# Expert routing and row scatter moved into the first attention layer's pipeline, in batches of four tiles

## What is computed

```
def _L0_ffn_ref(x, W1, b1, W2, b2, Wr, br):
    ...
    logits = xf @ Wr + br
    gates = jax.nn.softmax(logits, axis=-1)
    top_g, top_i = jax.lax.top_k(gates, K)          # E = 8, K = 2
    for e in range(E):
        w_e = jnp.sum(top_g * (top_i == e), axis=-1)
        h = jax.nn.gelu(xf @ W1[e] + b1[e], approximate=False)   # D = 192, I = 768
        out = out + w_e[:, None] * (h @ W2[e] + b2[e])
```

## Time and profile before

| | |
|---|---|
| median of 3 runs | 2311.49 us (2299.59 to 2316.12) |
| the profiled execution | 2312.43 us, span 2310.7 us |
| PE busy | 1958.2 us (85%) |
| DVE busy | 1397.8 us (60%) |
| ACT busy | 1011.0 us (44%) |
| POOL busy | 578.5 us (25%) |
| granted TensorE clock, mean | 0.914 of 2.4 GHz |

### The profile page before, as it was taken

The page is one execution under the profiler, slowest core; times in us unless marked ns, Lnnn a source line. Parts: engine busy times, 40 slices in busy tenths (PEclk is TensorE's granted clock), DMA queues, the critical chain, the costliest instruction groups (busy, mean ns, idle before and its releaser), DMA issues. The chain is left out here.

```text
span 2310.7 us, 57088 instructions
## 1 busy us (share of the span) xinstructions
PE 1958.2 (85%) x18472; PEld 1776.6 (77%) x18472; DVE 1397.8 (60%) x3149; ACT 1011.0 (44%) x2767; POOL 578.5 (25%) x1167
## 2 busy tenths in 40 slices
PE   5999999999500058999999999699999999999985
PEld 4888888888400058999999999588888888888872
DVE  5777777776432224555555554477777777777735
ACT  2555555555200022333333333366666666666631
POOL 4343333432057700000000000433333333333100
PEclk8999999999655578999999999599999999999957
DMA  4122222221012279788888886465555555555513
GB/s 130 56 58 59 62 55 62 56 60 34 10 59 78 78 197 267 219 239 234 235 235 235 235 233 200 118 179 163 160 158 157 156 162 162 162 161 159 152 30 109
DMA packets 377119, 322.00 MB, mean 139 GB/s; under 512 B 55432, under 2 KB 337760, under 8 KB 377058
## 3 DMA queue, kind: packets, MB, share of 16 engines
q1 hardware_dynamic: 357592, 287.49, 43.8%
q0 software_dynamic: 15360, 31.48, 4.5%
q10 hardware_dynamic: 4106, 2.24, 0.4%
HBM read 209.51 MB, written 111.60 MB: 139 GB/s over the span
## 5 line engine op out<-in xcount | busy, mean ns | idle before, releaser
L1122 ACT ACTIVATE prob<-ps_s,b1s 128x256 f32<-128x256 f32 x432 | 181.3, 471 | 371.6 <-PE ps_s L1106 371.6
L1106 PE MATMUL ps_s<-xhi,w1hi_c 128*128 128x256 f32 x864 | 240.1, 296 | 2.6 <-DVE xhi L1144 2.6
L1106 PE MATMUL ps_s<-xhi,w1lo_c 128*128 128x256 f32 x864 | 230.3, 284 | 0.0
L1081 PE MATMUL ps_v<-probT,prob 128*128 128x192 f32 x864 | 214.8, 331 | 0.0
L1069 PE MATMUL ps_t<-ident,xs 128*128 128x128 f32 x144 | 38.8, 295 | 207.2 <-DMA score<-w1h 206.4
L1081 PE MATMUL ps_k<-probT,prob 128*128 128x192 f32 x864 | 214.0, 330 | 0.0
L1136 DVE CAST w1hi_c<-score 128x768 fp32r<-128x768 f32 x144 | 74.1, 557 | 225.3 <-DMA score<-w1h 225.3
L371 PE MATMUL ps_k<-xT,wqk_c 128*128 128x128 f32 (+1 forms) x1408 | 198.7, 291 | 0.6 <-ACT xT L606 0.6
L422 PEld LDWEIGHTS ps_v<-vv,probT 128*128 128x128 f32 x1536 | 189.1, 199 | 1.1 <-issue 1.0
L422 PE MATMUL ps_v<-vv,probT 128*128 128x17 f32 x1536 | 187.7, 262 | 0.5 <-DVE hres L674 0.5
L1069 PEld LDWEIGHTS ps_t<-ident,xs 128*128 128x128 f32 x144 | 20.7, 144 | 215.3 <-DMA score<-w1h 206.0
(11 more groups left out here) (207 smaller groups left out, 4757.2 us busy)
## 6 DMA issues: line engine op xcount, KB each, us to landing
rel_d<-rpad SPq DMA_DIRECT2D x64, 864.0 KB, 4.4
relb<-rel_d SPq DMA_DIRECT2D x64, 768.0 KB, 5.1
probT<-w2h SPq DMA_DIRECT2D x72, 576.0 KB, 4.2
score<-w1h SPq DMA_DIRECT2D x72, 384.0 KB, 3.2
score<-w1h SPq DMA_DIRECT2D x144, 192.0 KB, 3.9
xs_d<-zrow SPq DMA_DIRECT2D x64, 216.0 KB
xs<-xs_d SPq DMA_DIRECT2D x72, 192.0 KB, 2.5
ys_d<-ys SPq DMA_DIRECT2D x72, 192.0 KB, 5.1
```

Of the source, the lines that this page charges most:

```text
L1081: last = pe.matmul(ps_y[s][:, 0:D], hT[b][:, c, s * 128:s * 128 + 128], w2[b][:, c, :], start=(c == 0), stop=(c == NI - 1))
L1106: last = pe.matmul(dst, w, x, start=(k == 0), stop=(k == len(terms) - 1))
L1122: last = act.activation(hT[b][:, c, :], ps_s[:, j, (c % 2) * BLK:(c % 2) * BLK + BLK], ACT.Gelu, bias=b1s[b][:, c:c + 1])
```

## The change

Blocks B and C are gone. Their work is done in block A for four tiles at a time:

- The ages grow to gate 11, pick 12, count 13, place 14, row 17, scatter 18; 20 steps are written out ahead of the loop instead of 12, and 18 behind it instead of 10. What is done for four tiles at once stands in every fourth step.
- DVE: `subtract_maximum` (2 instructions), `pick_experts` (15) and `place_rows` (9) stand at the end of a step's body, each once in four steps, on 128x32 or smaller operands. PE: `count_experts`, five matmuls behind the second half of the scores, which wait for `pick_experts`. ACT: an exponential of 128x32, a copy of the counts, and per tile the normalised row `srow` (before, DVE's work in block C). POOL: per tile two index copies and the two indirect stores, behind `rsz` and ahead of the next gather.
- Each expert has a fixed region of 8448 rows in `xs_d`, so that a row's place is known before all tokens are counted. The zeros written per tile are gone; four stores at the start zero 2048 spare rows, and eight at the start of block D zero the 256 rows behind each expert's last (`zero_tails`, on SP and ACT).
- Block D begins with a chain of DVE instructions for the tables `etabi` (expert) and `otabi` (first row of the block); SP now reads a second register per block, from `otabi`, behind the wait for the buffers. Packing the row numbers for the second layer and turning them is done in the first steps of block D.

```diff
+CAP = T * B + BLK
+ROWS = E * CAP + E * BLK
...
-AGES = [dict(gather=0, emb=1, ln=2, xn=3, qk=4, v=5, s=5, pt=6, o=7, y=8, z=9, lg=10),
+AGES = [dict(gather=0, emb=1, ln=2, xn=3, qk=4, v=5, s=5, pt=6, o=7, y=8, z=9, lg=10,
+             gate=11, pick=12, count=13, place=14, row=17, scatter=18),
...
+                if l == 0 and st.has("scatter"):
+                    t, j = st.tile("scatter"), st.four("scatter")
+                    after(pool, scat[j], 32 * st.quad("scatter"))
+                    pool.wait_ge(R_["placed"], st.quad("scatter") + 1)
+                    for k in range(TOPK):
+                        settle(pool, spare)
+                        pool.tensor_copy(sidx[j][k][:], posi[k][:, bass.ds(t, 1)]).then_inc(R_["idx"], 1)
+                    pool.wait_ge(R_["idx"], TOPK * upto(t))
+                    pool.wait_ge(R_["row"], upto(t))
...
+                        pool.indirect_dma_start(xs_d, bass.IndirectOffsetOnAxis(ap=sidx[j][k][:], axis=0),
+                                                srow[j][:], None).then_inc(scat[j], 16)
...
+                def count_experts():
+                    pe.wait_ge(R_["hots"], st.quad("count") + 1)
...
+                    pe.matmul(ps_t[:, 0:4 * E], tri_r[:], both_r[:], start=True, stop=False)
+                    for k in range(1, 4):
+                        pe.matmul(ps_t[:, k * E:4 * E], ones_r[:], both_r[:, 0:(4 - k) * E], start=False, stop=False)
+                    pe.matmul(ps_t[:, 4 * E:8 * E], ones_r[:], both_r[:], start=False, stop=True)\
...
+                if l == 0 and st.ends_quad("gate"):
+                    act.wait_ge(R_["less_max"], st.quad("gate") + 1)
+                    act.activation(gate4[:], gate4[:], ACT.Exp).then_inc(R_["gates"], 1)
+                if l == 0 and st.has("row"):
...
+                    act.activation(srow[j][:].rearrange("p (o d) -> p o d", o=1), hres[:, bass.ds(t, 1), :],
...
+                def pick_experts():
...
+                    rc.link(dve.tensor_reduce(gsum[:], gate4[:], AX.X, ALU.add))
+                    settle(dve, spare)
+                    rc.link(dve.reciprocal(gsum[:], gsum[:]))
+                    settle(dve, spare)
+                    rc.link(dve.tensor_tensor(gate4[:], gate4[:], wide(gsum[:]), ALU.mult))
+                    for k in range(TOPK):
+                        best, hot = quad_of("pick", wk[k]), one_hot[k]
+                        settle(dve, spare)
+                        rc.link(dve.tensor_reduce(best, gate4[:], AX.X, ALU.max))
+                        settle(dve, spare)
+                        rc.link(dve.tensor_tensor(hit[:], gate4[:], wide(best), ALU.is_equal))
+                        rc.link(dve.tensor_tensor(hit[:], hit[:], every(rev[:]), ALU.mult))
+                        settle(dve, spare)
+                        rc.link(dve.tensor_reduce(quad_of("pick", chosen[k]), hit[:], AX.X, ALU.max))
+                        settle(dve, spare)
+                        rc.link(dve.tensor_tensor(hot[:], hit[:], wide(quad_of("pick", chosen[k])), ALU.is_equal))
+                        if k == 0:
+                            rc.link(dve.scalar_tensor_tensor(gate4[:], hot[:], -2.0, gate4[:], ALU.mult, ALU.add))
+                    dve.tensor_tensor(both_r[:].rearrange("p (t e) -> p t e", e=E), one_hot[0][:], one_hot[1][:],
+                                      ALU.add).then_inc(R_["hots"], 1)
...
+                if l == 0 and st.ends_quad("gate"):
+                    subtract_maximum()
+                if l == 0 and st.ends_quad("pick"):
+                    pick_experts()
+                if l == 0 and st.ends_quad("place"):
+                    place_rows()
             pipeline(dve, ages, body, ch, 10 if l == 0 else 7)
...
+            for n in range(E * BLK // (128 * ZROWS)):
+                sp.dma_start(spare_rows[n], zrow[:, 0:ZROWS * D]).then_inc(xs_zero, 16)
...
-                    sp.dma_start(zr[bass.ds(t, 1)].rearrange("o p d -> (o p) d"), zrow[0:zr.shape[1], 0:ZROWS * D])\
-                        .then_inc(xs_zero, 16)
...
+                def block_row(t):
+                    return sp.value_load(otabi[0:1, bass.ds(t, 1)], min_val=0, max_val=ROWS - BLK)
...
                         after(sp, D_["h_sb"], NH * before2)
                         settle(sp, spare)
-                        rows_ = xs_d[bass.ds(t * BLK, BLK), :].rearrange("(s p) d -> p s d", s=2)
+                        rows_ = xs_d[bass.ds(block_row(t), BLK), :].rearrange("(s p) d -> p s d", s=2)
```

More of the change, by code:

```diff
@@ L237, in tower @@
         oT1 = two("oT1", [D1 + 1, 128])
-        srow = xn + zn
+        srow = four("srow", [128, D])
+        gate4 = sb("gate4", [128, 4, E])
+        gsum = sb("gsum", [128, 4])
+        hit = sb("hit", [128, 4, E])
+        one_hot = [sb(f"one_hot{k}", [128, 4, E]) for k in range(TOPK)]
+        both_r = sb("both_r", [128, 4 * E], F32R)
+        ranks = sb("ranks", [128, 8 * E])
+        place4 = sb("place4", [128, 4, E])
+        taken = sb("taken", [128, E])
+        filled = sb("filled", [128, E])
+        first_row = sb("first_row", [128, E])
+        rev = sb("rev", [128, E])
         w1 = [[score[p][:].rearrange("p g a k -> p (g a k)")[:, c * I:(c + 1) * I] for c in range(2)]
@@ L273, in tower @@
         xs_zero = sem("xs_zero")
+        scat = [sem(f"scat{p}") for p in range(SCAT)]
         rel_zero = sem("rel_zero")
@@ L278, in tower @@
                  "mvz_ok", "rsz_ok", "zn_ok", "zT_ps", "zT_sb", "lg_ps", "lg_sb")
+        R_ = {n: sem("R_" + n) for n in ("table", "dve", "less_max", "gates", "hots", "ranks_ps", "ranks_sb", "placed",
+                                         "row", "idx")}
         L = [{n: sem(f"L{l}_{n}") for n in NAMES} for l in range(2)]
@@ L571, in body @@
                                    ACT.Copy).then_inc(S["q_sb"], 1)
+                if l == 0 and st.ends_quad("count"):
+                    act.wait_ge(R_["ranks_ps"], st.quad("count") + 1)
+                    after(act, R_["placed"], st.quad("count"))
+                    act.activation(ranks[:], ps_t[:, 0:8 * E], ACT.Copy).then_inc(R_["ranks_sb"], 1)
                 if st.has("qk"):
@@ L666, in embed_and_normalise, with quad_of, wide, every @@
                         dve.bn_aggr(mv[be][:], st6[be][:]).then_inc(S["mv_ok"], 1)
+                def quad_of(k, tensor):
+                    return tensor[:, bass.ds(4 * st.quad(k), 4)]
+                def wide(ap):
+                    return ap.rearrange("p (t o) -> p t o", o=1).to_broadcast([128, 4, E])
+                def every(ap):
+                    return ap.rearrange("p (o e) -> p o e", o=1).to_broadcast([128, 4, E])
+                def subtract_maximum():
+                    q = st.quad("gate")
+                    rc.base, rc.at = ROUTE_STEPS * q, 0
+                    dve.wait_ge(S["lg_sb"], upto(st.tile("gate")))
+                    settle(dve, spare)
+                    part = logits[:, bass.ds(4 * q, 4), 0:E]
+                    rc.link(dve.tensor_reduce(gsum[:], part, AX.X, ALU.max))
+                    settle(dve, spare)
+                    dve.tensor_tensor(gate4[:], part, wide(gsum[:]), ALU.subtract).then_inc(R_["less_max"], 1)
@@ new lines, in place_rows @@
+                def place_rows():
+                    q = st.quad("place")
+                    rc.base, rc.at = ROUTE_STEPS * q, 15
+                    dve.wait_ge(R_["ranks_sb"], q + 1)
+                    settle(dve, spare)
+                    rc.step(dve.tensor_tensor(place4[:], ranks[:, 0:4 * E].rearrange("p (t e) -> p t e", e=E),
+                                              every(filled[:]), ALU.add))
+                    rc.link(dve.tensor_reduce(taken[:], ranks[:, 4 * E:8 * E].rearrange("p (t e) -> p e t", e=E),
+                                              AX.X, ALU.add))
+                    rc.step(dve.tensor_tensor(filled[:], filled[:], taken[:], ALU.add))
+                    for k in range(TOPK):
+                        rc.link(dve.tensor_tensor(hit[:], one_hot[k][:], place4[:], ALU.mult))
+                        settle(dve, spare)
+                        rc.link(dve.tensor_reduce(quad_of("place", posf[k]), hit[:], AX.X, ALU.add))
+                        settle(dve, spare)
+                        rc.link(dve.tensor_copy(quad_of("place", posi[k]), quad_of("place", posf[k])))
+                    settle(dve, spare)
+                    assert rc.at == ROUTE_STEPS, rc.at
+                    dve.sem_inc(R_["placed"], 1)
@@ L1111, in _ @@
             def _(act):
+                act.wait_ge(B_["tables"], 1)
+                zero_tails(act, range(1, E, 2))
                 def body(st):
+                    if isinstance(st.n, int) and st.n == 4:
+                        act.wait_ge(B_["turned_ps"], 1)
+                        act.activation(turned[:].rearrange("n q k -> n (q k)"), ps_q[0:NT, :], ACT.Copy)\
+                            .then_inc(B_["turned"], 1)
                     if st.has("h"):
```

256 lines of the change are left out of this document (126 added, 130 removed).

## The result

| | before | after |
|---|---|---|
| median of the runs, us | 2312.9 (6 runs, 2299.59 to 2317.88) | 2507.73 (6 runs, 2491.04 to 2545.86) |
| ratio, 95% interval | | 1.083 (1.077 to 1.088): slower |
| span of the profiled execution, us | 2310.7 | 2512.8 |
| mean granted clock | 0.914 | 0.833 |
| last `zn` group of block A | 612.1 | 902.0 |

What follows compares the result with a forecast made beforehand. PE and the DVE-POOL loop were taken as level in block A, without slack. Terms -156.5 + 108 + 10 + 5 + 3 + 18 + 37 = +24.5 on 2312.4 gave 2336.9, so 2336 us; range 2262 to 2395.

Steps and rivals of the forecast that it cites:

- the hole: Between block A's last zn and block D's first load: scatters move into block A, load at 660.7 not 817.2, -156.5 us.
- DVE's additions: Block A: 26 routing instructions, 8.3 us per four tiles at the end of DVE's step, uncovered, 13 groups: +108 us.
- PE's clock: Block A's picking steps: PE's pauses drop its clock for 20 us in two groups of three, 4.3 us each: +37 us.
- drain, ACT, start: DVE's work in block A's drain +10, ACT's exponential holding softmax back +5, zeroing spare rows at the start +3.
- block D: SP's extra register load behind the wait for h_sb, 0.55 us per block, half paid over 64 steps: +18 us.
- the 30 that the prediction had named as a sign against itself: End of block A: scatters trailing the pipeline by more than 30 us would show the forecast wrong.
- the factor of 1.8: Block A, PE: key matmuls take 2.93 us at the low clock against 1.60 at the high one.
- the idle of some 4 us in a picking step: Block A, PE: 4.2 us idle beside DVE's longer picking step, in three pieces of 1.0 to 1.7 us.
- Rival C: Block A: clock falls in every picking step and does not rise before the next, 13 x 18 = 238: 2537 us; chance 0.06.
- Links: DVE's chained instructions: a plain link adds 0.04 us, one with settle 0.15; the skill's rule would make the sum 30 smaller.

Runs made afterwards that it cites:

- the burst alone: Kernel before plus 20 chained 128x32 DVE operations at the end of every fourth step of block A: 2693.45 us (before: 2354.27).
- the burst with a row of fillers: Kernel before plus 20 chained DVE operations every fourth step and 14 unused 128x128 matmuls in PE's step behind each: 2407.07 us (before: 2359.5).
- fillers in the changed kernel: Changed kernel plus 5 unused 128x128 matmuls in every block A step and 10 more behind each pick_experts: 2373.43 us, ratio 1.007.
- the spread version: Changed kernel with routing split over four steps ahead of zn, ACT's row and block D's register load moved earlier: ratio 1.059, without settle 1.029.
- the fillers' row of 14: Changed kernel plus 23 unused matmuls (3, 14 and 6) where PE paused, once in four steps; the 14 stand ahead of the sums: ratio 1.058.
- the first run without routing: Changed kernel without pick_experts, count_experts and place_rows, row numbers fixed ahead of block A, scatters and ACT's rows kept: 2528.21 us.
- the short burst: Kernel before plus 6 chained 128x32 DVE operations at the end of every fourth step of block A: 2351.29 us (before: 2359.5).
- the spread version without fillers: Changed kernel, routing split over four steps without the 13 settle, ACT's row and block D's register load moved, no filling matmuls: ratio 1.029.

## Why the prediction was wrong

| term | forecast | measured |
|---|---|---|
| the hole | -156.5 | -150.6 |
| DVE's additions | +108 | +113 = 13 x (43.8 - 35.1) |
| PE's clock | +37 | +179 = 598 / 62.5 x (62.5 - 43.8) |
| drain, ACT, start | +18 | -2, what is left of block A's 289.9 |
| block D | +18 | +61 |
| rest | 0 | +1 |
| sum | +24.5 | +202.1 |

**The hole** was right: 54.5 us, of which the last store came 32.6 us behind the last `zn`, where the forecast had 29.4, and the rest took 22 as against 19. (32.6 is just over the 30 that the prediction had named as a sign against itself; the hole came out right even so.)

**DVE** was right, though only the stretches at clock 1.00 show it: `pick_experts` 4.8 us (forecast 4.9), four steps 43.8 (forecast 43.3). The step that picks takes 14.35 us (forecast near 13.5), the others 8.7 to 9.1 and, with `place_rows`, 11.7.

**The step that failed is the term for PE's clock:** a fall in two groups of three, 20 us low each time, 4.3 us per group. That it falls behind `pick_experts` was right for four of the six falls; the two behind `place_rows` were not foreseen. Right were also the factor of 1.8 (62.5 us for four steps against 4 x 8.65 = 34.6) and the idle of some 4 us in a picking step (forecast 4.2, measured 2.8 from 133 to 141 and 4.0 from 411 to 422). What was wrong is how long it stays low. I took 20 us from 32 to 52 us and 23 from 1476 on the earlier trace rows, two stretches at the edges of a stage, and called them long. In the steady steps it stayed low for 27 to 147 us, six times, and in the runs with a burst or without routing for 700 to 850. So 598 us were low and not the 13 x 2/3 x 20 = 173 of the forecast, and the term was 179 and not 37. Fewer falls, each far longer. That this is the cause is shown by runs: the burst alone makes the kernel before 339 us longer (2693.45 against 2354.27), the burst with a row of fillers 48 (2407.07 against 2359.5), and fillers in the changed kernel take it from 2546.41 to 2373.43 on one chip, although they add work to its bound. Not shown is what decides how long a low stretch lasts.

Rival C had the mechanism and nearly the length of a low cycle (61.6 us forecast, 62.5 measured): 2537 against 2508. That it came so near is in part luck: it has block A at +364 where it was +290, since the clock did rise five times, and block D at +18 where it was +61. I gave it 0.06, because from 52 us on the clock of the kernel before did rise. That counted against C one rise, in a stage that was still filling. The range left it out, and that was the mistake in the working of the chances: nothing in the trace of before bounded the length of a low stretch in steady attention, since there was none, and a cost that no row shows has to be bounded from the far side.

**Block D** was mis-sized in its second half. The extra register load costs 0.64 us (0.55 forecast). But it is paid in full and not by half: PE's idle time in the stage went from 623.3 - 584.9 = 38.4 us to 684.5 - 599.5 = 85.0, and 46.6 / 72 = 0.65 per block (72 blocks, where the sum counted 64). Each longer wait also costs clock (0.95 against 0.97), and PE is busy for 14.6 us more with the same work. Together 61.

**Links.** A link with `settle` starts 0.33 us behind the last and one without 0.23 (410.50, 410.83 and 411.06 above), so the increment costs 0.1 us. The Trainium skill ("VectorE: DVE Perf Modes", "The DRAIN you can't avoid") has eight copies take the same time with a semaphore after each as with one after the last. Here every link has such an increment and a wait, at 0.23 us; what costs 0.1 is a separate increment instruction set between two links, which that comparison does not cover. So the page and the rows do not contradict each other, and the prediction was wrong to take the page as a price for both kinds. Without the 13 increments, spread routing went from a ratio of 1.059 to 1.029, part of it by a later fall of the clock.

## What to carry to other kernels

Before work is put on an engine that TensorE waits for, look at the pauses it makes and not at its mean length: where TensorE runs without a gap at the high clock, a pause of one to three microseconds can cost hundreds (here shorter ones did too, at 229, 349 and, in the spread version, 161 us), and the profile then shows a TensorE that is 100% busy and looks like an honest bound; the granted clock in the same row tells. Price a low clock by a run in which it falls in the stage concerned, or by the whole stage, not by a stretch from elsewhere. And a few idle matmuls in TensorE's waits, or an address load moved ahead of a wait, are cheap to try: here they gained some 125 us of the whole and 59 us of block D.

## What the hardware showed that I had not expected

In attention either level of TensorE's clock can last. At 1.2 GHz the steps keep PE busy without a gap (845 of 847 us in the run with the burst), and that alone did not bring the clock back. Where it came back, a row of full-size matmuls stood just before: the fillers' row of 14 in the run above, and in the changed kernel all five times the 12 key matmuls and the transposes behind them, the densest row of a step. Three of the five had the counting matmuls ahead as well. The rises at 216 and 376 us, from PE's timeline:

```profile
211.77 2.93 PE L414 MATMUL ps_k<-xT,wqk_c 128*128 128x128 f32 x12
```

```profile
214.00:215.00 1.00, 1.00 (x7) 0.93 (x5) 0.33 (x1) 0.27 (x1) 1.00 (x1) 0.50 0.23 54
215.00:216.00 1.00, 1.00 (x16) 0.69 (x15) 0.00 (x0) 0.71 (x2) 0.01 (x1) 0.80 0.23 61
```

```profile
371.31 0.40 PE L497 MATMUL ps_t<-both_r,tri_r 128*128 128x32 f32 x1
...
372.39 2.91 PE L414 MATMUL ps_k<-xT,wqk_c 128*128 128x128 f32 x12
```

Such a row stands in every step, and most did nothing; what decides when one does is open. So is why pauses of the same size were sometimes survived. In the kernel after, 0.82, 0.64 and 0.52 us between 393 and 398 us and 1.02 at 402 were, and 0.88, 0.65 and 0.52 between 224 and 229 were not. In the first run without routing one of 1.05 us at 165 was, and one of 1.04 at 199 was not. The mean busy share did not tell either: the short burst held the clock at 225 of 240 us, and the spread version without fillers lost it at 115 of 120.
